# Down product of eight chunks in three fp32r passes, router steps a slot later, in the last layer of a one-core decoder kernel

## The reference

```python
logits = h @ gate_w.T;  scores = sigmoid(logits)
# top 8 of 32 experts within the 4 best of 8 groups, normalised, times 2.5 -> combine (tokens x 32)
g = silu(einsum('th,eih->tei', h, w_gate));  u = einsum('th,eih->tei', h, w_up)
routed = einsum('tei,ehi->th', g * u * combine[:, :, None], w_down)
shared = (silu(h @ sh_gate.T) * (h @ sh_up.T)) @ sh_down.T
x = x + routed + shared
```

## Time and profile before

| | us |
|---|---|
| median of 3 runs | 703.51 |
| the profiled execution | 704.8 |
| its span, from the first to the last instruction | 703.1 |
| TensorE busy | 650.8 |
| VectorE busy | 491.2 |
| ScalarE busy | 379.8 |
| GpSimd busy | 340.7 |
| mean granted TensorE clock | 0.982 of full speed |

### The profile page before, as it was taken

How to read it: one execution, slowest core, us unless ns; L and a number is a source line. 1 busy time by engine, 2 the same in 40 slices (tenths; PEclk the granted TensorE clock), 3 DMA queues, 4 the chain that set the end, 5 groups by cost and what they waited for, 6 DMA issues and landing times.

```text
span 703.1 us, 11039 instructions
## 1 busy us (share of the span) xinstructions
PE 650.8 (93%) x3466; PEld 467.1 (66%) x3466; DVE 491.2 (70%) x1262; ACT 379.8 (54%) x699; POOL 340.7 (48%) x418
## 2 busy tenths in 40 slices
PE   8978788877689999999988999999999999999997
PEld 8645555544578888888776666666666666666663
DVE  4687788999516666666667687768595767858573
ACT  3674677663129999999843634343534444343221
POOL 6134788777874655566348665452708153000000
PEclk9998999998999999999999999999999999999999
DMA  9920040000144677765121845644545354534370
GB/s 230 334 84 1 15 124 35 32 31 31 46 133 127 186 223 210 203 185 165 46 62 34 199 92 133 157 103 126 133 120 145 110 143 119 132 97 121 109 187 22
DMA packets 74871, 84.14 MB, mean 120 GB/s; under 512 B 15345, under 2 KB 43995, under 8 KB 74814
## 3 DMA queue, kind: packets, MB, share of 16 engines
q1 hardware_dynamic: 69688, 74.93, 39.0%
q0 software_dynamic: 4288, 8.40, 4.0%
q10 hardware_dynamic: 838, 0.11, 0.1%
HBM read 64.48 MB, written 18.87 MB: 119 GB/s over the span
## 4 chain that ended last, share of the span: by engine, by line
PE 65%; DVE 9%; POOL 7%; issue 4%; DMA 2%; ACT 2%; DVEq 0%; ACTq 0%; SPq 0%
PE pair_banks L1721 16%; PE bank L1488 10%; PE bank L1490 10%; PE bank L1489 10%; PE pair_banks L1390 4%; PE score_banks L1490 4%; PE score_banks L1489 4%; PE score_banks L1488 4%; POOL yg L634 3%; POOL x_sorted L553 2%; DVE xsb L1125 2%; DVE smax L1139 2%; DMA yg<-y_sorted,posi 1%; DVE ssum L1131 1%; PE bank L1528 1%
## 5 line engine op out<-in xcount | busy, mean ns | idle before, releaser
L905 ACT ACTIVATE r_s<-bank 128x512 f32<-128x512 f32 x136 | 80.9, 598 | 149.7 <-PE bank L1490 148.3
L1721 PE MATMUL pair_banks<-t_s,Dn 128*128 128x512 f32 x272 | 137.2, 592 | 0.6 <-DVE t_s L1324 0.6
L1316 DVE TENSOR_TENSOR rc_s<-r_s,score_banks 128x512 f32<-128x512 f32 x90 | 61.6, 684 | 51.7 <-ACT r_s L905 48.3
L1488 PE MATMUL bank<-fxh,Gh 128*128 128x512 f32 x136 | 93.8, 690 | 0.0
L1329 DVE TENSOR_TENSOR t_s<-rc_s,bcb 128x512 f32<-128x512 f32 x128 | 88.5, 693 | 1.4 <-PE pair_banks L1721 0.8
L634 POOL DMA_INDIRECT yg<-y_sorted,posi x64 | 64.0, 999 | 30.8 <-issue 18.4
L553 POOL DMA_INDIRECT x_sorted<-xsb,posi x64 | 63.9, 999 | 26.3 <-DVE xsb L1125 14.6
L1721 PEld LDWEIGHTS pair_banks<-t_s,Dn 128*128 128x128 f32 x272 | 51.3, 189 | 16.4 <-issue 5.3
L1211 DVE TENSOR_TENSOR h1l<-score_banks,h1h 128x512 fp32r<-128x512 f32 x46 | 31.8, 691 | 31.6 <-ACT score_banks L851 31.6
L1490 PE MATMUL bank<-fxh,Gl 128*128 128x512 f32 x136 | 53.7, 395 | 0.0
L1489 PE MATMUL bank<-fxl,Gh 128*128 128x512 f32 x136 | 53.7, 395 | 0.0
(11 more groups left out here) (314 smaller groups left out, 1688.8 us busy)
## 6 DMA issues: line engine op xcount, KB each, us to landing
bcb<-c_rows SPq DMA_DIRECT2D x128, 256.0 KB, 4.1
wraw<-in_L_xattn_W SPq DMA_DIRECT2D x46, 256.0 KB
x_sorted<-wraw SPq DMA_DIRECT2D x1, 5888.0 KB, 17.5
xg<-x_sorted SPq DMA_DIRECT2D x23, 256.0 KB, 3.5
y_sorted<-ysb SPq DMA_DIRECT2D x23, 256.0 KB, 2.8
ctxb<-in_ctx SPq DMA_DIRECT2D x8, 256.0 KB, 5.7
out<-x_all SPq DMA_DIRECT2D x8, 256.0 KB, 4.3
x_all<-in_x SPq DMA_DIRECT2D x2, 512.0 KB, 4.8
```

Source lines behind the costliest of these rows:

```text
L905: act.activation(r_s[:, n % RB2, :], bank[n % 3][:, :], ACT.Silu).then_inc(F["act"], 1)
L1316: tt(rc_s[:, n % CB2, :], r_s[:, n % RB2, :], bank[3 + n % 3][:, :], ALU.mult).then_inc(F["rc"], 1)
L1488: mm(dst, wh, xh, start=start, stop=False)
L1721: mm(bank[6][:, :], Dn[:, weights_of(p), :], t_s[:, n % TB2, :], start=(p == 0), stop=(p == NC2 - 1))\
```

## The change

Eight chunks (5 to 12) of supertiles 1 to 6 get their down product in three fp32r passes instead of one fp32 product. For this the down weights of these chunks are also kept as high and low halves (`Dh`, `Dl`, weight groups 9 and 10: one more ScalarE copy and one more VectorE subtraction each), and `t_s` is split three slots after it was made (`SPLIT`): ScalarE writes the high half (`high_t`), VectorE the low half (`low_t`), into 5 buffers each. `LAG2` goes from 3 to 6 and `t_s` gets 8 buffers instead of 6. For all supertiles `lg`, `back`, `sc` and `rt_a` to `rt_d` come a slot later, `c_ps` and `cT` a slot earlier (14), `accS`, `tp` and `x2` three slots later (14, 15, 16). The guards of bank 7 are set anew: `to_tokens` waits for `cT` instead of `sc`, `prep_x` for `x2` of three supertiles before, `prep_c` no longer for `x2`. Two pairs of semaphores are merged.

```diff
-LAG2, RB2, CB2, TB2 = 3, 4, 11, 6
+LAG2, RB2, CB2, TB2 = 6, 4, 11, 8
+SPLIT, HB2, HALVES = 3, 5, range(5, 13)
-SLOTS = dict(cmbA=-3, cmbB=-3, paggr=-2, prstd=-2, pnb=0, pxn=1, pxT_ps=3, pxT=3, fxl=4, lg=5, lgS=5, back=6, sc=7, rt_a=8,
-             rt_b=9, rt_c=10, rt_d=11, c_ps=15, cT=15, accS=11, tp=12, x2=13)
+SLOTS = dict(cmbA=-3, cmbB=-3, paggr=-2, prstd=-2, pnb=0, pxn=1, pxT_ps=3, pxT=3, fxl=4, lg=6, lgS=6, back=7, sc=8, rt_a=9,
+             rt_b=10, rt_c=11, rt_d=12, c_ps=14, cT=14, accS=14, tp=15, x2=16)
+def halved_at():
+
+    steps, k = {}, 0
+    for n, some in weighted_at().items():
+        here = [m for m in some if m % NC2 in HALVES and 1 <= m // NC2 < NS - 1]
+        steps[n + SPLIT] = [(m, k + i) for i, m in enumerate(here)]
+        k += len(here)
     return steps
...
-            for g in (*range(8), NG - 1):
+            for g in (*range(8), 9, 10, NG - 1):
...
+            def high_t(m, k):
+                act.wait_ge(F["t"], m + 1)
+                if k >= HB2:
+                    act.wait_ge(F["dn"], halves[k - HB2] + 1)
+                copy(t_h[:, k % HB2, :], t_s[:, m % TB2, :]).then_inc(F["th"], 1)
...
+                    for m, k in halved.get(n, ()):
+                        high_t(m, k)
                     if n >= EARLY:
                         silu(n)
...
+                    if g in (9, 10):
+                        at = slice((g - 9) * 4, (g - 8) * 4)
+                        dve.wait_ge(s_f2h, g)
+                        tt(Dl[:, at, :], f2_bank(g), Dh[:, at, :].bitcast(F32), ALU.subtract)
...
+            def low_t(m, k):
+                dve.wait_ge(F["th"], k + 1)
+                if k >= HB2:
+                    dve.wait_ge(F["dn"], halves[k - HB2] + 1)
+                tt(t_l[:, k % HB2, :], t_s[:, m % TB2, :], t_h[:, k % HB2, :].bitcast(F32), ALU.subtract)\
+                    .then_inc(F["tl"], 1)
...
                     for m in steps[n]:
                         weighted(m)
+                    for m, k in halved.get(n, ()):
+                        low_t(m, k)
...
-                mm(bank[6][:, :], Dn[:, weights_of(p), :], t_s[:, n % TB2, :], start=(p == 0), stop=(p == NC2 - 1))\
-                    .then_inc(F["dn"], 1)
+                if n in halves:
+                    k = halves.index(n)
+                    pe.wait_ge(F["tl"], k + 1)
+                    w = p - HALVES[0]
+                    ins = three(bank[6][:, :], Dh[:, w, :], Dl[:, w, :], t_h[:, k % HB2, :],
+                                t_l[:, k % HB2, :], start=False, stop=False)
+                else:
+                    ins = mm(bank[6][:, :], Dn[:, weights_of(p), :], t_s[:, n % TB2, :], start=(p == 0),
+                             stop=(p == NC2 - 1))
+                ins.then_inc(F["dn"], 1)
...
                 if j + 2 < NS:
-                    pe.wait_ge(F["sc"], j + 3)
+                    pe.wait_ge(F["cT"], j + 3)
...
+                if j >= 3:
+                    pe.wait_ge(F["x2"], j - 2)
...
                 pe.wait_ge(F["cw"], j + 1)
-                if j >= 2:
-                    pe.wait_ge(F["x2"], j - 1)
```

More of the change, by code:

```diff
@@ L108, in weighted_at @@
     assert done == NS * NC2
+    return steps
+def halved_at():
[4 more added lines that the diff above has]
+        k += len(here)
     return steps
@@ L263, in decoder_kernel @@
             Dn = a("Dn", [P, NC2, P])
+            Dh, Dl = (a(n, [P, len(HALVES), P], F32R) for n in ("Dh", "Dl"))
+            t_h, t_l = (a(n, [P, HB2, ST], F32R) for n in ("t_h", "t_l"))
             yg = a("yg", [P, 2, TPS, 2, D])
@@ L301, in decoder_kernel @@
         s_ident, s_consts = sem("ident"), sem("consts")
-        s_vzero = sem("values_zeroed")
-        s_zsrc, s_zero = sem("zeros_made"), sem("scratch_zeroed")
+        s_zeros, s_zero = sem("zeros_made"), sem("scratch_zeroed")
         s_w = [sem(f"expert_in{i}") for i in range(WB)]
@@ L314, in decoder_kernel @@
             "ctx_transposed", "ctxT", "router1_logits", "router1_logits_read", "router1_logits_back", "router1_logits_kept"))
-        s_shift, s_exp1 = sem("router1_shifted"), sem("router1_exp")
+        s_exp1 = sem("router1_exp")
         s_picked, s_rank, s_pos, s_eb = (
@@ L328, in decoder_kernel @@
         F = {n: sem("f2_" + n) for n in (
-            "up gate act rc t dn accS tp x2 cmb1 cmb bst pstat prstd pnb pxn pxT_ps fxh xT fxl lg lgS back sc cw c_ps cT "
+            "up gate act rc t th tl dn accS tp x2 cmb1 cmb bst pstat prstd pnb pxn pxT_ps fxh xT fxl lg lgS back sc cw c_ps cT "
             "chain pxv").split()}
@@ L385, in _ @@
             sp.wait_ge(s_ctx[NQ - 1], 32)
-            sp.wait_ge(s_zsrc, 1)
+            sp.wait_ge(s_zeros, 2)
             sp.dma_start(xs_v.rearrange("b p t d -> p b (t d)"),
@@ L517, in _ @@
             pool.memset(one[:, :], 1.0)
-            pool.memset(vf[:, :, :, :, :], 0.0).then_inc(s_vzero, 1)
-            pool.memset(wraw[:, WB - 1, 0, :], 0.0).then_inc(s_zsrc, 1)
+            pool.memset(vf[:, :, :, :, :], 0.0).then_inc(s_zeros, 1)
+            pool.memset(wraw[:, WB - 1, 0, :], 0.0).then_inc(s_zeros, 1)
             pool.iota(rev[:, :], pattern=[[-1, E1]], base=E1, channel_multiplier=0,
@@ L772, in head @@
                     if m == 0:
-                        act.wait_ge(s_vzero, 1)
+                        act.wait_ge(s_zeros, 1)
                     if m >= 2:
@@ L818, in _ @@
                 if n == 7:
-                    act.wait_ge(s_shift, 1)
+                    act.wait_ge(s_picked, 2)
                     act.activation(second[:, :, :], second[:, :, :], ACT.Exp).then_inc(s_exp1, 1)
@@ L888, in acc_out @@
                 copy(accS[:, :], bank[6][:, :]).then_inc(F["accS"], 1)
-            for g in (*range(8), NG - 1):
+            for g in (*range(8), 9, 10, NG - 1):
                 act.wait_ge(s_f2ps, g + 1)
-                for hi, lo, part in f2_dst(g):
+                for hi, lo, part in f2_dst(g) if g not in (9, 10) else [(Dh[:, (g - 9) * 4:(g - 8) * 4, :], None, slice(0, 4))]:
                     ins = copy(hi, f2_bank(g)[:, part, :])
@@ L905, in silu @@
                 act.activation(r_s[:, n % RB2, :], bank[n % 3][:, :], ACT.Silu).then_inc(F["act"], 1)
+            halved = halved_at()
+            def high_t(m, k):
[3 more added lines that the diff above has]
+                copy(t_h[:, k % HB2, :], t_s[:, m % TB2, :]).then_inc(F["th"], 1)
+            halves = [m for some in halved.values() for m, _ in some]
             for n in range(EARLY):
@@ L1042, in router1_picked @@
                 tt(lgt[:, :, :], pick[:, :, :], pick2[:, :, :], ALU.add).then_inc(s_picked, 1)
-                tt(second[:, :, :], second[:, :, :], best[:, :, :], ALU.subtract).then_inc(s_shift, 1)
+                tt(second[:, :, :], second[:, :, :], best[:, :, :], ALU.subtract).then_inc(s_picked, 1)
             def router1_counts():
@@ L1220, in _ @@
                 else:
-                    dve.wait_ge(s_f2h, g + 1 if g < 8 else 9)
+                    dve.wait_ge(s_f2h, g + 1 if g < 8 else 11)
                     for hi, lo, part in f2_dst(g):
@@ L1367, in _ @@
             gated(2)
-            steps = weighted_at()
+            def low_t(m, k):
[4 more added lines that the diff above has]
+                    .then_inc(F["tl"], 1)
+            steps, halved = weighted_at(), halved_at()
+            halves = [m for some in halved.values() for m, _ in some]
             for i in range(NS):
@@ L1696, in _ @@
                 ins.then_inc(s_f2ps, 1)
+            halves = [m for some in halved_at().values() for m, _ in some]
             def weights_of(p):
```

## The result

The changed kernel takes 702.42 us (median of 9 runs, 700.11 to 704.34), the kernel before 703.86 in runs beside it (9 runs, 702.79 to 706.94). Their ratio is 0.9967, 95% interval 0.9951 to 0.9982: faster by 2.3 us, 1.3 to 3.4. Forecast were 3.4 us, so the direction held and the gain is some 1 us short. The profiled execution took 700.28 us, its span 698.5.

A forecast was written before the change was run, and what follows sets the result against it. TensorE's own work was taken to bound the steady supertiles, with supertile 0 waiting on VectorE and GpSimd. Terms of -9.5, +2.6 and +3.5 sum to -3.4 us, from the median 703.5 to 700.1 us; range 696.3 to 702.9.

The forecast's parts named there:

- Term 1: TensorE's down products: three fp32r passes take 0.68 instead of 0.88 us, 0.197 saved on each of 48, -9.5 us.
- Term 2: Supertile 0: LAG2 of 6 leaves three down products to be made later at full rate, +2.6 us.
- Term 3: Router's end: TensorE waits 0.7 us for cw in supertiles 2 to 6, 0.1 in supertile 1, together +3.5 us.
- Rival 1: Router's end: TensorE does not wait for cw, so 696.6 us; chance 0.14.
- Rival 2: Supertile 0 costs nothing because VectorE is served earlier, so 697.5 us; chance 0.08.
- Rival 3: Slots 0 to 7: VectorE becomes the bound through slow low halves, kernel slower, 705.6 us at 1.5 each; chance 0.08.
- Rival 4: Down products: three passes between fp32 ones get no cheaper, still 0.88 us, so 706.7 us; chance 0.04.
- edits taken at nothing: Split halves on ScalarE and VectorE, later logits and x2, weight groups, merged semaphores: all covered by slack, 0 us.

The follow-up runs named there:

- e4_nosplit: Changed kernel with no t_s split, every down product one fp32 product, weight halves still made: 708.24 us, ratio 1.0044 to the kernel before.
- e1_c15: Changed kernel with the combine weights transposed in slot 15 instead of 14, tp and x2 after them: 697.99 us, ratio 0.9902 to the kernel before.
- e3_late: Changed kernel with Dh and Dl made from Dn in slots 2 to 5 of supertile 1, not in the weight stage: 701.21 us, ratio 0.9958.
- e2_tile0: Changed kernel with down products of chunks 0 to 10 of supertile 0 three slots behind their weighting, all others six: 701.61 us, ratio 0.9961.
- e5_all: Changed kernel, cw transposed in slot 15, supertile 0's chunks 1 to 10 three slots behind, weight halves made in supertile 1; second chip: 705.37 against 718.04 us.
- g5_all: Changed kernel, cw transposed in slot 15, supertile 0's chunks 1 to 10 three slots behind, weight halves made in supertile 1; third chip: 706.93 against 717.17 us.
- e8_filler: Changed kernel with five more `unread` products while TensorE waits for the last low halves of the weights, on another chip: 712.58 us.
- g6_tile0b: Changed kernel with down products of chunks 1 to 10 of supertile 0 three slots behind their weighting, chunk 0 six, on another chip: 712.26 us.
- e7_router: Changed kernel with the router's steps back in their old slots (5 to 11), cw read in slot 14, on another chip: 731.5 us.
- g7_router: Changed kernel with the router's steps back in their old slots (5 to 11), cw read in slot 14, repeated on another chip: 725.9 us.

## Why the prediction was right, and where it was not

By the traces of the first chip the last layer's difference splits into four terms. Each is read as the difference of two kernels that follow each other, so that they add up to the whole is no test of them; what stands for each by itself is said behind the table.

| term | forecast | measured | from |
|---|---|---|---|
| 48 split products | -9.5 | -9.27 | e4_nosplit to e1_c15, cw1 to end |
| waits for cw, supertiles 2 to 6 | +3.5 | +3.01 | after to e1_c15, cw1 to end |
| supertile 0's three down products | +2.6 | +2.63 | before to e4_nosplit, cw1 to end |
| ahead of cw1: weight groups 9 and 10 | 0 | +0.89 | cw1 behind the first gather, before to after; 0.77 of it goes in e3_late, 0.12 stays unexplained |
| sum | -3.4 | -2.74 | 345.43 to 342.69 |

The kernels timed on this chip go the same way by their ratios: e4_nosplit +3.1 (trace +3.5), e3_late -3.0 (-3.6), e2_tile0 -2.7 (-3.2), e1_c15 -6.9 (-5.8), the change -2.3 (-2.7).

**Term 1** held: 0.193 a product for 0.197, since the three passes join the six beside them without a gap. Its far bound, a pass of 0.171, and the 131 ns of the Trainium skill ("TensorE: Matmul & The Clock Gate", Back-to-back issue gap) did not show: passes start 0.227 apart. By the slots alone it is 2.245 - 2.04 = 0.20 a product.

**Term 2** held in size and cause: TensorE stood idle in supertile 0 for what it did not have to do, and made it later, at the end of the kernel. That these are the three products, and nothing else in the new schedule, is shown by e5_all and g5_all, which give back 2.66 and 2.64.

**Term 3** held in mechanism. cw ended 481.37 - 477.81 = 3.56 behind slot 12's down product, where 3.76 was forecast. The difference is in rt_d's slot, 481.29 - 478.49 = 2.80 where the sum took 520.94 - 517.92 = 3.02: 0.25 of that was an idle stretch of VectorE, which is not there now. It cost 0.60 each, not 0.7. One thing for readers of wait lists: the list names 0.34 for such a wait. The transposing came 0.50 later than 477.81 + 3.12 and the period is 0.58 longer; the likely reason, not shown, is that part of a wait hides under the end of the matmul before it, which is modelled.

**The step that failed** is "Weight groups 9 and 10: two subtractions more on VectorE, 1.2 us, in front of a wait of 1.27 for gathered rows that stays", taken at nothing. For VectorE the cover held. Its timeline in the changed kernel still has a wait for gathered rows, now 0.74:

```profile
367.24 0.74 DVE L1364 SCALAR_TENSOR_TENSOR x_all<-yg,wts,x_all 128x128 f32<-128x128 f32 x2 [0.74 <-DMA yg<-y_sorted,posi]
```

But TensorE waits for the same subtractions at `pe.wait_ge(s_f2l, NG)`, and I had asked only who is behind them on VectorE. Its idle time grew by 1.2, the granted clock of the products that follow was 0.50 to 0.55, and a fixed number of products at that clock ran past the moment when nb was ready. e3_late took the two subtractions away; the wait was 1.64 again, the second stretch had the full clock, and 0.77 of the 0.89 went with them. So that the two weight groups cost this on the first chip is shown. That the longer idle time is what lowers the clock is not: all four executions with it on that chip had 0.50 to 0.57 in the six microseconds from 363, but three of four on the other chips kept 1.00, and the run meant to part the two (e8_filler) was inconclusive. That the range held in spite of this step is in part luck: the term was small, and term 3 came out 0.5 us better than forecast.

**The rivals.** Rival 1, no wait for cw, did not hold in the changed kernel; e1_c15 is what it would have been: without the wait the period is 38.32, against 38.3 forecast. Rival 2 fell with e4_nosplit. Rival 3, VectorE late from contention, did not come, though its cause is there: single low halves took up to 1.225 us, but the median is 0.686 and the mean 0.736. In slot 7 of supertile 2 VectorE is 0.8 us late (its product starts at 468.08, the silu that it reads ends at 466.68 + 0.60), by one low half of 1.22 just before. In slot 8 nothing of that is left, and VectorE even has idle time again, behind the table loads:

```profile
470.81 0.69 DVE L1343 TENSOR_TENSOR rc_s<-r_s,bank 128x512 f32<-128x512 f32 x1 [1.42 <-ACT r_s L917]
```

Rival 4 fell with the 0.68 of three passes. The other edits taken at nothing hold in the steady supertiles: e4_nosplit's period, with all of them but the split of t_s, is 39.86 against 39.84, and e1_c15's 38.32 is 1.54 below it, where eight slots of 2.04 instead of 2.245 give 1.6.

## What to carry to other kernels

Work put into a stage "behind a wait that stays" has to be followed to every engine that waits for it, and an engine made to wait there can come back slower. The same subtractions that VectorE had time for cost 0.8 us through TensorE on the first chip. Half the clock followed the longer wait in all four executions there and in one of four on the two others. A schedule step whose margin is worked out as negative by 0.7 us can be moved before it is built: one slot for cw was worth 3 us, more than the whole change (by the traces 339.61 against 342.69 for the last layer; the medians, 697.99 against 702.42, differ by 4.4). Work taken out of a stretch in which an engine waits for others isn't saved but postponed, and is paid for where that engine is the bound.

## What the runs showed of the hardware

- A VectorE operation with two SBUF inputs beside GpSimd's work took up to 1.225 us instead of 0.69 (low halves), and 48 more of them went with a mean weighting of 702 instead of 693 ns. The Trainium skill ("GPSIMD Engine Reference", Specifications) has the contention without a size; here it was 50 ns on the mean of the low halves, and it was absorbed.
- Two waits of 1.12 and 1.09 us close together (e2_tile0) were followed by granted clocks of 0.91, 0.50 and 0.74 in the three stretches of 2 us from 384 to 390. Waits of 1.01 and 1.14 that lay 6.5 us apart (after, 383.35 and 389.85) were followed by 1.00 up to 392, and single waits of 0.3 to 0.5 in the steady supertiles by no lower clock.
- A wait of TensorE of the same length, 2.83 or 2.84 us, at the same place was followed by a granted clock of 0.50 to 0.57 between 363 and 369 on one chip (after, e1_c15, e2_tile0, e4_nosplit) and by 1.00 in g6_tile0b, e7_router and g7_router on two others.
- On two of three chips ScalarE waited 6.18 (e5_all) to 7.86 us (e8_filler) in supertile 0 of the last layer, in every kernel, for what the profile calls remote; on the first chip there was no such wait. The steady period of the kernels with cw in slot 15 was the same on all of them (38.32 and 38.33).
